# Reading the attention's stacked heads in sixteen-row pieces, and taking the combining weights' split one step earlier

## The chip, the cores and the metric

The kernel runs on one core of one Trainium2 chip. The metric is the device time of one execution in microseconds (us), lower is better. The program is one launch that computes two layers one after the other, so every stage's time adds to the total.

## The reference, cut to what matters

Eight batches of 512 tokens with 256 channels pass through four stages, each added to its input: an attention, a mixture of eight experts, a state-space block, and a second mixture of experts. The change touches the first and the last.

```python
xq, xk, xv = (x @ w.T + b).reshape(b, h, t, d)      # 16 heads of 16 channels, a reshape, not a transpose
xq, xk = rotate(xq), rotate(xk)                     # folded into the weights by the kernel
p = softmax(einsum('bhqd,bhkd->bhqk', xq, xk) / sqrt(d)); o = einsum('bhqk,bhkd->bhqd', p, xv)
...
p = softmax(maximum(x @ gate_W + gate_b, 1e-4))     # second mixture
w = maximum(p, 0.1) for the two best experts, divided by their sum
out = einsum('bsef,bse->bsf', einsum('bsd,edf->bsef', x, expert_W) + expert_b, w) / 2
```

## The kernel before, in words

Each engine runs one instruction stream; streams meet at semaphores, and an instruction that waits holds up all that stand behind it on its engine.

**Attention.** It runs in slots `t`, one for each of 32 tiles (a batch n has four; tile u = 4n + r holds four heads). Products of queries and keys are made of an upper and a lower part of each operand, three products in one matmul: a stack has 48 rows for each head pair, 16 rows each of "upper, lower, upper" against "lower, upper, upper". In slot t:

- SP, the queue that issues most transfers, first reads the stacks of tile t+3 (`load_stack`, which calls `read_stack` for two halves) when the transposed scores of slot t-1 are issued, then a tile of x (`load_rows`, L285), then stores the negated row maxima of tile t+1 (`load_maxima`, L318), waits for that store to land, and reads them into the stack (L322, two transfers). The scores of slot t+1 wait for these. Then it writes chunk t+8 of the projected queries or keys to the scratch tensor `scr` in HBM, an upper and a lower part (`write_scratch`, L263), each of 2048 pieces of 128 bytes. In every fourth slot a transfer of 512 KB of the residual follows (L379 or L340).
- TensorE takes the transposed scores of tile t (L928, sixteen matmuls), the scores of tile t+2 for the maxima (L937), the values, projections and transposes.
- VectorE takes the maxima (L670), ScalarE the exponentials (L523), GpSimd the splits into parts (L452, L454, L444, L446).

In slots -5 to -1 the same SP order holds for the first tiles; ACT issues half of tile 0's stack reads.

**Second mixture.** For each of eight batches there are 16 units, four token tiles by four pairs of experts. TensorE makes a unit in six matmuls of 512 columns (L1922) in one of four PSUM banks. Even units are weighed and added by VectorE (`accumulate`, L1820, two instructions), odd ones by ScalarE (L1684) and GpSimd (L1564). Unit u on an even bank may start when VectorE is done with unit u-4. Between its accumulations for batch n VectorE works out the combining weights of batch n+1, each step waiting for the one before: `shares` after unit 10, `share_parts` after unit 12. The result of `share_parts` is used by TensorE after unit 3 of batch n+1 (L1892), that of `shares` by ScalarE from unit 1 of it on.

```python
            for u in range(0, L.UNITS, 2):
                self.accumulate(n, u)
...
                else:
                    wait(pe, S["acc_done"], L.UNITS // 2 * n + u // 2 - 1)
```

Of the kernel before, what the change touches and what calls it, by code (L numbers as in the profile page):

```python
# [10 lines left out]
F32 = mybir.dt.float32  # L11
# [13 lines left out]
def wait(eng, sem, value):  # L25

    if not isinstance(value, int) or value > 0:
        eng.wait_ge(sem, value)
# [44 lines left out]
class Experts:  # L73
# [14 lines left out]
    def carve(self, k, at, shape, dt=F32, n=1):  # L88

        size = int(np.prod(shape[1:]))  # L90
        part = self.w[:, k:k + n, :] if dt == F32R else self.plain_pair[:, :, :] if n == 2 else self.plain[k][:, 0:1, :]
        flat = part.rearrange("p e c -> p (e c)")[:, at:at + size]
        names = ["a", "b", "c", "d"][:len(shape) - 1]
        return flat.rearrange(f"p ({' '.join(names)}) -> p {' '.join(names)}", **dict(zip(names, shape[1:])))
# [38 lines left out]
def attention_phase(nc, all_sems, A, x_out, route, experts):  # L133

    with ExitStack() as ctx:
# [30 lines left out]
        qst = carve(2, 0, [P, 4, 2, 512], F32R)  # L166
        kst = carve(3, 0, [P, 4, 2, 512], F32R)
# [22 lines left out]
        both, before = sb("both", [P, E0, 5]), sb("before", [P, E0, 5])  # L190
# [14 lines left out]
        scr = nc.dram_tensor("at_scr", (2, 2, 2, DK, NH, NJ, 32), F32, kind="Internal").ap()  # L205
# [16 lines left out]
        stack_ready = [sem(f"stack_ready{r}") for r in range(4)]  # L222
# [36 lines left out]
        def write_scratch(eng, q, kind):  # L259

            n, a = q // 4, q % 4
            to = scr[n % 2, a // 2, (kind + a // 2) % 2, :, :, 8 * (a % 2):8 * (a % 2) + 8, :].rearrange("d h j k -> j d h k")
            eng.dma_start(to, (qk_hi, qk_lo)[kind][:, q % 2, :].bitcast(F32)).then_inc(scr_written[n % 2][a % 2], 16)  # L263

        def read_stack(eng, u, half):

            r, n = u % 4, u // 4
            for b in range(2):
                eng.wait_ge(scr_written[n % 2][b], 64 * (n // 2 + 1))
            heads = slice(4 * r + 2 * half, 4 * r + 2 * half + 2)  # L270
            row = 64 * half
            for m, st, pair, single in ((0, qst, 16, 0), (1, kst, 0, 32)):
                both = scr[n % 2, m, :, :, heads].rearrange("s d h j k -> (s d) (h j k)")
                eng.dma_start(st[row + pair:row + pair + 32, r, :, :].bitcast(F32).rearrange("d h n -> d (h n)"), both).then_inc(stack_ready[r], 16)
                upper = scr[n % 2, m, m, :, heads].rearrange("d h j k -> d (h j k)")
                eng.dma_start(st[row + single:row + single + 16, r, :, :].bitcast(F32).rearrange("d h n -> d (h n)"), upper).then_inc(stack_ready[r], 16)

        def chunk_bank(q):
            return t_ps[:, q % 2, :] if q < 4 else f_ps[:, :]
# [1 line left out]
        def sync(sp):  # L281
# [22 lines left out]
            def load_stack(u):  # L304

                if u == 0:
                    sp.wait_ge(const_set, 5)
                wait(sp, t_ready, 16 * (u - 3))
                read_stack(sp, u, 0)
                if u:  # L310
                    read_stack(sp, u, 1)
# [13 lines left out]
            def write_chunk(q):  # L325

                n, a = q // 4, q % 4
                if a == 0:
                    for r in range(4):
                        wait(sp, stack_ready[r], 128 * (n - 1))  # L330
                sp.wait_ge(qk_hi_ready, q + 1)
                write_scratch(sp, q, 0)
                if q > 3:
                    sp.wait_ge(qk_lo_ready, q + 1)
                    write_scratch(sp, q, 1)
# [6 lines left out]
            for t in SLOTS:  # L342
# [8 lines left out]
                if (q := chunk(t)) is not None:  # L351
                    write_chunk(q)
                    if q == 3:
                        load_stack(0)
# [30 lines left out]
            for k in range(E0):  # L385
                at = sp.value_load(pad_row[0:1, k:k + 1], min_val=0, max_val=LIST - P)
# [107 lines left out]
        def scalar(act):  # L494
# [15 lines left out]
            def first_chunk(q):  # L510

                act.wait_ge(qk_ready, q + 1)
                if q > 1:
                    act.wait_ge(scr_written[0][q % 2], 32)
                act.activation(qk_hi[:, q % 2, :], qk[:, q % 2, :], ACT.Copy).then_inc(qk_hi_ready, 1)
                act.wait_ge(qk_lo_ready, q + 1)
                write_scratch(act, q, 1)
# [40 lines left out]
            for t in SLOTS:  # L558
# [5 lines left out]
                for k in range(16):  # L564
# [26 lines left out]
                    if k == 15 and t == -5:  # L591
                        read_stack(act, 0, 1)
# [321 lines left out]
        def tensor(pe):  # L914
            pe.wait_ge(ident_in, 16)

            def of_head(stack, r, h, rows, chunk=None):

                half = slice(64 * (h // 2), 64 * (h // 2) + rows)
                return stack[half, r, h % 2, :] if chunk is None else stack[half, r, h % 2, chunk * P:(chunk + 1) * P]  # L920
# [9 lines left out]
            def scores(u, m, a):  # L930

                if m == 0 and a == 1:
                    pe.wait_ge(stack_ready[u % 4], 128 * (u // 4 + 1))
                if a == 1:
                    wait(pe, max_done, 8 * u + m - 1)
                h, c = m // 4, m % 4
                last = pe.matmul(s_ps[:, m % 2, a, :], of_head(qst, u % 4, h + 2 * a, 48, c), of_head(kst, u % 4, h + 2 * a, 48), start=True, stop=True)  # L937
                if a == 0:
                    last.then_inc(s_ready, 1)
# [82 lines left out]
            for t in SLOTS:  # L1022
# [3 lines left out]
                for k in range(16):  # L1026
                    if tile(t) is not None:
                        scores_T(t, k)
                    if (u := tile(t + 2)) is not None:
                        scores(u, k // 2, 1 - k % 2)  # L1030
# [10 lines left out]
                    if k in (4, 6) and (n := batch(t, 10)) is not None:  # L1041
# [3 lines left out]
                        h = (k - 4) // 2  # L1045
# [24 lines left out]
            n = NB - 2  # L1070
# [366 lines left out]
class SecondExperts:  # L1437

    E, PAIRS, XB = 8, 4, 4
# [51 lines left out]
class SecondSync:  # L1491
# [21 lines left out]
    def body(self):  # L1513

        L, S, sp = self.L, self.L.S, self.sp
        for n in range(NB):
            sp.wait_ge(S["tile_done"], 4 * (n + 1))
            sp.dma_start(self.x_out[n * T:(n + 1) * T, :].rearrange("(k p) c -> p k c", p=P), L.x[n % L.XB][:, :, :]).then_inc(S["x_stored"], 16)
            if n + L.XB < NB:
                sp.wait_ge(S["x_stored"], 16 * (n + 1))  # L1520
                self.load(n + L.XB)
        sp.wait_ge(S["x_stored"], 16 * NB)
# [190 lines left out]
class SecondVector:  # L1713
# [73 lines left out]
    def shares(self, n):  # L1787

        L, S, dve, steps, E = self.L, self.L.S, self.dve, self.top_steps, self.L.E
        m0, m1, c, left = L.work  # L1790
        comb = L.comb[n % 2]
        wait(dve, S["odd_done"], L.UNITS * (n - 1))
        steps(dve.scalar_tensor_tensor(m1, L.p, 0.1, m0, ALU.max, ALU.mult))
        steps(dve.tensor_reduce(L.small[:, 0, :], m1, AX.X, ALU.add))
        steps(dve.reciprocal(L.small[:, 1, :], L.small[:, 0, :]))
        steps(dve.tensor_tensor(m1, m1, self.per_row(L.small[:, 1, :]), ALU.mult))
        dve.tensor_scalar(comb, m1, 0.5, None, ALU.mult).then_inc(S["comb_ready"], 1)

    def share_parts(self, n):

        L, S, dve, steps, E = self.L, self.L.S, self.dve, self.top_steps, self.L.E
        comb = L.comb[n % 2]
        upper, lower, again = (L.comb_3[:, :, r * E:(r + 1) * E] for r in range(3))
        dve.wait_ge(S["comb_ready"], n + 1)
        wait(dve, S["combT_ps"], n)
        steps(dve.tensor_copy(upper.bitcast(F32R), comb))
        dve.tensor_copy(again, upper)
        dve.tensor_tensor(lower, comb, upper, ALU.subtract).then_inc(S["comb_3_ready"], 1)
        assert steps.count == L.TOP_STEPS, steps.count
# [17 lines left out]
    def first_batch(self):  # L1827

        self.dve.wait_ge(self.L.S["const_in"], 48)
        self.scores(0)  # L1830
        self.first_choice(0)
        self.second_choice(0)
        self.shares(0)
        self.share_parts(0)

    def body(self):

        L, dve = self.L, self.dve
        for n in range(NB):
            dve.wait_ge(L.S["comb_ready"], n + 1)  # L1840
            for u in range(0, L.UNITS, 2):
                self.accumulate(n, u)
                if n + 2 < NB:
                    if u == 0:
                        self.variance(n + 2)
                    if u == 2:
                        self.newton(n + 2)
                if n + 1 < NB:
                    if u == 6:
                        self.scores(n + 1)  # L1850
                        self.first_choice(n + 1)
                    if u == 8:
                        self.second_choice(n + 1)
                    if u == 10:
                        self.shares(n + 1)
                    if u == 12:
                        self.share_parts(n + 1)


class SecondTensor:  # L1860
# [630 lines left out]
```

## Time and profile before

| what | value |
|---|---|
| median of 3 runs | 2147.16 us (2144.86 to 2148.03) |
| profiled execution, its own time | 2147.16 us |
| span from first to last instruction | 2145.3 us |
| mean granted TensorE clock | 0.94 |
| busy: TensorE, VectorE, ScalarE, GpSimd | 88%, 76%, 60%, 66% |

The time outside the span is 1.9 us. A share of busy time is a mean over four stages with different limits; what a change is worth has to be read in its own stage. Line numbers are those of the kernel printed above. SPq is SP's queue of transfer issues; its durations are the time that the issue took, not the transfer.

### The profile page before, as it was taken

The numbers are of one execution on the slowest core, as the hardware profiler recorded it, in microseconds if no ns is written. First come the engines' busy times: TensorE is split into PE (matmuls) and PEld (weight loads), VectorE is DVE, ScalarE is ACT, GpSimd is POOL, SyncE is SP. The second block draws the span as 40 slices with busy tenths as digits, with TensorE's granted clock in tenths as the row PEclk, the third lists the DMA queues.
The fourth block names the chain that finished last, engine by engine and source line by source line (L and its number), as shares of the span: only waits on it lengthen the run. The fifth ranks groups of instructions, "written<-read, shape, count | busy, mean of one in ns | idle before, by whom it ended". The sixth has DMA issues, their size and how long they took to land.

```text
span 2145.3 us, 32281 instructions
## 1 busy us (share of the span) xinstructions
PE 1894.8 (88%) x9878; PEld 1109.1 (52%) x9878; DVE 1641.0 (76%) x2274; ACT 1283.0 (60%) x2736; POOL 1421.8 (66%) x1198
## 2 busy tenths in 40 slices
PE   3699999999973999984799999999999999779998
PEld 2344444444433999982345353535454544247776
DVE  4688888787744655650699999999999999966664
ACT  3177666676662433335687777777777767734443
POOL 4344445542334344440699999999999999966665
PEclk8599999998885999996899999999999999999999
DMA  5666656555235454560404050405040404200100
GB/s 105 117 108 107 100 101 117 116 116 112 65 116 176 81 92 72 115 138 23 168 0 178 0 178 0 178 0 178 1 178 0 168 0 169 98 30 21 40 30 30
DMA packets 231395, 194.35 MB, mean 91 GB/s; under 512 B 147219, under 2 KB 200235, under 8 KB 230716
## 3 DMA queue, kind: packets, MB, share of 16 engines
q1 hardware_dynamic: 205498, 163.33, 28.9%
q0 software_dynamic: 13296, 17.77, 4.8%
q10 hardware_dynamic: 12434, 11.18, 1.9%
q8 instruction: 85, 1.39, 0.3%
q14 instruction: 82, 0.67, 0.1%
HBM read 138.15 MB, written 54.08 MB: 90 GB/s over the span
## 4 chain that ended last, share of the span: by engine, by line
POOL 34%; PE 12%; issue 7%; ACT 1%; DVE 1%; DMA 0%; POOLq 0%; DVEq 0%; ACTq 0%
POOL mb_dbu L2110 22%; POOL mb_hp L2116 10%; PE mb_da_ps L1922 9%; POOL mb_dtu L2122 1%; PE mb_f_ps L1883 1%; PE mb_f_ps L2352 1%; PE mb_f_ps L2370 0%; PE mb_y_ps L1901 0%; PE mb_f_ps L2356 0%; PE mb_f_ps L2360 0%; PE mb_f_ps L1872 0%; DVE mb_da_ps L2292 0%; DVE mb_hp L2290 0%; ACT mb_res L2186 0%; ACT mb_xin L2189 0%
## 5 line engine op out<-in xcount | busy, mean ns | idle before, releaser
L2110 POOL TENSOR_TENSOR mb_dbu<-mb_dtu,mb_bbc 128x1024 f32<-128x1024 f32 x256 | 598.8, 2363 | 3.6 <-DVE mb_hp L2290 1.5
L523 ACT ACTIVATE ex_plain<-at_t_ps 128x512 f32<-128x512 f32 x512 | 289.4, 595 | 175.0 <-PE at_t_ps L928 169.6
L2292 DVE TENSOR_TENSOR_SCAN mb_da_ps<-mb_da_ps,mb_dbu 128x1024 f32<-128x1024 f32 x160 | 365.4, 2284 | 4.6 <-ACT mb_da_ps L2164 3.3
L2333 PE MATMUL mb_y_ps<-mb_hc,lw_ident 128*128 128x512 f32 x640 | 311.4, 609 | 41.8 <-DVE mb_hc L2299 41.4
L670 DVE TENSOR_REDUCE at_mx<-at_s_ps 128x2 f32<-128x1024 f32 x256 | 310.6, 1218 | 35.0 <-PE at_s_ps L937 33.1
L937 PE MATMUL at_s_ps<-ex_w 48*128 48x512 f32 x512 | 226.4, 505 | 24.1 <-DVE at_mx L670 23.9
L928 PE MATMUL at_t_ps<-ex_w 64*128 64x512 f32 x512 | 219.0, 485 | 12.2 <-ACT ex_plain L523 7.0
L2116 POOL TENSOR_TENSOR mb_hp<-mb_hp,mb_cbc 128x1024 f32<-128x1024 f32 x96 | 226.5, 2359 | 0.0
L2290 DVE TENSOR_TENSOR_SCAN mb_hp<-mb_da_ps,mb_dbu 128x1024 f32<-128x1024 f32 x96 | 218.9, 2280 | 8.9 <-POOL mb_dbu L2110 6.3
L1309 POOL DMA_INDIRECT x<-m_o,m_xs x71 | 113.2, 1594 | 162.6 <-DMA x<-m_o,m_xs 88.3
L2333 PEld LDWEIGHTS mb_y_ps<-mb_hc,lw_ident 128*128 128x128 f32 x640 | 117.7, 191 | 199.4 <-issue 126.1
L2299 DVE TENSOR_TENSOR mb_hc<-mb_da_ps,mb_cbc 128x1024 f32<-128x1024 f32 x160 | 195.4, 1221 | 12.5
L2333 PE MATMUL mb_y_ps<-mb_hp,lw_ident 128*128 128x512 f32 x384 | 186.1, 608 | 15.6 <-POOL mb_hp L2116 15.6
L928 PEld LDWEIGHTS at_t_ps<-ex_w 64*128 64x128 f32 x512 | 86.4, 192 | 171.1 <-ACT ex_plain L523 125.9
L2163 ACT ACTIVATE mb_da_ps<-mb_dt,lw_a_neg 128x512 f32<-128x512 f32 x256 | 172.6, 674 | 0.0
L2164 ACT ACTIVATE mb_da_ps<-mb_dt,lw_a_neg 128x511 f32<-128x511 f32 x256 | 171.9, 672 | 0.0
L2162 ACT ACTIVATE mb_da_ps<-mb_zero 128x1 f32<-128x1 f32 x256 | 43.0, 168 | 204.1 <-DVE mb_hc L2299 162.4
L1414 PE MATMUL m_y_ps<-ex_w,m_xsT_hi 128*128 x568 | 157.0, 337 | 0.1
L948 PE MATMUL at_o_ps<-ex_plain 128*32 128x512 f32 x1024 | 144.6, 638 | 0.1
L1564 POOL TENSOR_TENSOR m_odd<-m_odd,m_odd_in 128x256 f32<-128x256 f32 x96 | 70.8, 737 | 95.7 <-ACT m_odd_in L1684 91.2
L2333 PEld LDWEIGHTS mb_y_ps<-mb_hp,lw_ident 128*128 128x128 f32 x384 | 73.6, 195 | 106.6 <-issue 76.5
L1820 DVE SCALAR_TENSOR_TENSOR m_x<-mb_da_ps,m_small,m_x 128x256 f32<-128x256 f32 x128 | 61.8, 483 | 81.0 <-PE mb_da_ps L1922 78.2
(354 smaller groups left out, 4088.6 us busy)
## 6 DMA issues: line engine op xcount, KB each, us to landing
mb_bbc<-mb_scr SPq DMA_DIRECT2D x64, 512.0 KB, 6.0
mb_cbc<-mb_scr SPq DMA_DIRECT2D x64, 512.0 KB, 6.0
ex_w<-at_scr SPq DMA_DIRECT2D x126, 128.0 KB, 3.6
m_xs<-rt_rows SPq DMA_DIRECT2D x71, 129.0 KB
at_scr<-at_qk_hi SPq DMA_DIRECT2D x32, 256.0 KB
ex_w<-at_scr SPq DMA_DIRECT2D x126, 64.0 KB, 3.6
at_scr<-at_qk_lo SPq DMA_DIRECT2D x28, 256.0 KB
at_xin<-in_x SPq DMA_DIRECT2D x32, 128.0 KB, 4.0
```

What stands on the lines that cost most here:

```text
L523: act.activation(probs[:, c, h, :], t_ps[:, k % 2, :], ACT.Exp, scale=SCALE).then_inc(exp_done, 1)
L670: dve.tensor_reduce(out, s_ps[:, m % 2, :, :], AX.X, ALU.max).then_inc(max_done, 1)
L928: pe.matmul(t_ps[:, k % 2, :], of_head(kst, r, h, 64, c), of_head(qst, r, h, 64), start=True, stop=True).then_inc(t_ready, 1)
L937: last = pe.matmul(s_ps[:, m % 2, a, :], of_head(qst, u % 4, h + 2 * a, 48, c), of_head(kst, u % 4, h + 2 * a, 48), start=True, stop=True)
L1922: last = pe.matmul(L.o_ps[:, u % 4, :], rows, w[:, e, kt, :], start=(m == 0), stop=(m == 5))
L2110: pool.tensor_tensor(dbu[:, q % 3, :, :], dtu_2, bbc[:, 2 * p:2 * p + 2, :], ALU.mult).then_inc(S["dbu_ready"], 1)
L2116: pool.tensor_tensor(hp[:, r, :, :], hp[:, r, :, :], cbc[:, 2 * p:2 * p + 2, :], ALU.mult).then_inc(S["hp_ready"], 1)
L2163: act.activation(da_ps[:, q % 2, 0, :], dt[:, d % 2, :], ACT.Exp, scale=a_neg[:, d, 2 * p:2 * p + 1])
L2290: dve.tensor_tensor_scan(hp[:, t % 3, :, :].rearrange("p j t -> p (j t)"), da, add, 0.0, ALU.mult, ALU.add).then_inc(S["scan_done"], 1)
L2292: dve.tensor_tensor_scan(da, da, add, 0.0, ALU.mult, ALU.add).then_inc(S["scan_done"], 1)
L2299: dve.tensor_tensor(hc[:, t % 2, :, :], da_ps[:, r, :, :], cbc[:, 2 * p:2 * p + 2, :], ALU.mult).then_inc(S["hc_ready"], 1)
L2333: last = pe.matmul(y_ps[:, v % 2, :], ident[:, :], src[:, j, :], start=False, stop=(q == tile_last[v] and j == 1))
```

## The change

Two edits. In the attention, the scratch tensor is laid out by part and operand, and each half of a tile's stacks is read by six transfers of 16 rows (64 KB) where four transfers were used before, two of 32 rows and two of 16. The rows, and the bytes, are the same; the key stack's order becomes "upper, upper, lower" and the query stack's "upper, lower, upper", which gives the same three products. The counts that TensorE and SP wait for rise from 128 to 192 for each tile. In the second mixture, the three instructions of `share_parts` are moved to the end of `shares`, so they stand before the accumulation of unit 12, not after it.

```diff
-            to = scr[n % 2, a // 2, (kind + a // 2) % 2, :, :, 8 * (a % 2):8 * (a % 2) + 8, :].rearrange("d h j k -> j d h k")
+            to = scr[n % 2, kind, a // 2, :, :, 8 * (a % 2):8 * (a % 2) + 8, :].rearrange("d h j k -> j d h k")
...
-            heads = slice(4 * r + 2 * half, 4 * r + 2 * half + 2)
-            row = 64 * half
-            for m, st, pair, single in ((0, qst, 16, 0), (1, kst, 0, 32)):
-                both = scr[n % 2, m, :, :, heads].rearrange("s d h j k -> (s d) (h j k)")
-                eng.dma_start(st[row + pair:row + pair + 32, r, :, :].bitcast(F32).rearrange("d h n -> d (h n)"), both).then_inc(stack_ready[r], 16)
-                upper = scr[n % 2, m, m, :, heads].rearrange("d h j k -> d (h j k)")
-                eng.dma_start(st[row + single:row + single + 16, r, :, :].bitcast(F32).rearrange("d h n -> d (h n)"), upper).then_inc(stack_ready[r], 16)
+            for kind, m, st, at in ((0, 0, qst, 0), (0, 0, qst, 32), (0, 1, kst, 0), (0, 1, kst, 16), (1, 0, qst, 16), (1, 1, kst, 32)):
+                row = 64 * half + at
+                eng.dma_start(st[row:row + 16, r, :, :].bitcast(F32).rearrange("d h n -> d (h n)"),
+                              scr[n % 2, kind, m, :, 4 * r + 2 * half:4 * r + 2 * half + 2].rearrange("d h j k -> d (h j k)")).then_inc(stack_ready[r], 16)
...
-                        wait(sp, stack_ready[r], 128 * (n - 1))
+                        wait(sp, stack_ready[r], 192 * (n - 1))
...
-                    pe.wait_ge(stack_ready[u % 4], 128 * (u // 4 + 1))
+                    pe.wait_ge(stack_ready[u % 4], 192 * (u // 4 + 1))
...
         dve.tensor_scalar(comb, m1, 0.5, None, ALU.mult).then_inc(S["comb_ready"], 1)
-
-    def share_parts(self, n):
-
-        L, S, dve, steps, E = self.L, self.L.S, self.dve, self.top_steps, self.L.E
-        comb = L.comb[n % 2]
-        upper, lower, again = (L.comb_3[:, :, r * E:(r + 1) * E] for r in range(3))
         dve.wait_ge(S["comb_ready"], n + 1)
         wait(dve, S["combT_ps"], n)
         steps(dve.tensor_copy(upper.bitcast(F32R), comb))
...
                     if u == 10:
                         self.shares(n + 1)
-                    if u == 12:
-                        self.share_parts(n + 1)
```

## Rows read from the trace of the kernel before

**Rows 1.** The four stages, by windows: busy time, clock, DMA share, GB/s
```profile
95.00:640.00 545.00, 506.03 (x4432) 230.09 (x4430) 420.55 (x712) 364.48 (x739) 234.90 (x357) 0.93 0.53 104
980.00:1925.00 945.00, 851.09 (x2257) 411.39 (x2258) 852.38 (x585) 684.89 (x1424) 872.07 (x455) 0.97 0.24 87
1925.00:2145.30 220.30, 213.17 (x1009) 169.37 (x1007) 134.64 (x387) 94.51 (x210) 132.17 (x167) 0.99 0.10 32
```

**Rows 2.** Waits of SP's queue, 95 to 510 us: total, times, longest
```profile
SPq L322 <- DMA at_nscr<-at_nm_parts: 84.3, 25, 5.0
SPq L274 <- PE at_t_ps L928: 32.1, 20, 3.5
SPq L263 <- POOL at_qk_hi L452: 28.7, 16, 5.2
```

**Rows 3.** Timeline of SP, slot 1: start us, us, what
```profile
112.16 1.77 SPq L274 DMA_DIRECT2D ex_w<-at_scr  x1
113.98 0.41 SPq L276 DMA_DIRECT2D ex_w<-at_scr  x1
...
116.75 0.42 SPq L276 DMA_DIRECT2D ex_w<-at_scr  x1
117.21 0.42 SPq L285 DMA_DIRECT2D at_xin<-in_x  x1
117.68 0.43 SPq L318 DMA_DIRECT2D at_nscr<-at_nm_parts  x1
121.19 0.52 SPq L322 DMA_DIRECT2D ex_w<-at_nscr  x2
```

**Rows 4.** Timeline of SP, a store of maxima with nothing ahead of it
```profile
589.32 0.32 SPq L318 DMA_DIRECT2D at_nscr<-at_nm_parts  x1
590.75 0.53 SPq L322 DMA_DIRECT2D ex_w<-at_nscr  x2
```

**Rows 5.** Timeline of SP: the reads of maxima in slots -1, 3, 4, 7
```profile
92.11 0.53 SPq L322 DMA_DIRECT2D ex_w<-at_nscr  x2
...
152.35 0.52 SPq L322 DMA_DIRECT2D ex_w<-at_nscr  x2
...
166.79 0.53 SPq L322 DMA_DIRECT2D ex_w<-at_nscr  x2
...
213.76 0.52 SPq L322 DMA_DIRECT2D ex_w<-at_nscr  x2
```

**Rows 6.** Timeline of PE: first transposed scores of slots 0, 4, 5, 8
```profile
95.00 0.40 PE L928 MATMUL at_t_ps<-ex_w 64*128 64x512 f32 x1
...
155.93 0.40 PE L928 MATMUL at_t_ps<-ex_w 64*128 64x512 f32 x1
...
170.60 0.40 PE L928 MATMUL at_t_ps<-ex_w 64*128 64x512 f32 x1
...
217.03 0.40 PE L928 MATMUL at_t_ps<-ex_w 64*128 64x512 f32 x1
```

**Rows 7.** Timeline of VectorE, second mixture, units 10 to 14 of batch 2
```profile
2005.09 0.18 DVE L1797 TENSOR_SCALAR m_small<-m_small 128x32 f32<-128x32 f32 x1
2005.18 1.00 DVE L1820 SCALAR_TENSOR_TENSOR m_x<-mb_da_ps,m_small,m_x 128x256 f32<-128x256 f32 x2
2006.10 0.51 DVE L1806 CAST m_small<-m_small 128x32 fp32r<-128x32 f32 x1
2006.64 0.18 DVE L1807 COPY m_small<-m_small 128x32 f32<-128x32 f32 x1
2006.74 0.19 DVE L1808 TENSOR_TENSOR m_small<-m_small 128x32 f32<-128x32 f32 x1
2006.84 1.00 DVE L1820 SCALAR_TENSOR_TENSOR m_x<-mb_da_ps,m_small,m_x 128x256 f32<-128x256 f32 x2
```

**Rows 8.** Timeline of GpSimd and PE in the same stretch
```profile
2005.09 0.78 POOL L1579 TENSOR_TENSOR m_x<-m_x,m_odd 128x256 f32<-128x256 f32 x1
2005.84 0.73 POOL L1564 TENSOR_TENSOR m_odd<-m_odd,m_odd_in 128x256 f32<-128x256 f32 x1
2006.94 0.39 PE L1922 MATMUL mb_da_ps<-lw_next_hi,m_xT_hi 128*128 128x512 f32 x1
```

**Rows 9.** Timeline: two small VectorE steps and the GpSimd operations beside them
```profile
1999.73 1.43 POOL L1571 TENSOR_TENSOR m_odd<-m_odd,m_bias 128x256 f32<-128x256 f32 x2
2000.07 0.44 DVE L1781 TENSOR_TENSOR m_small<-m_small 128x32 f32<-128x32 f32 x1
2000.55 0.66 DVE L1782 TENSOR_TENSOR m_small<-m_small 128x32 f32<-128x32 f32 x1
```

**Rows 10.** Timeline: VectorE's maxima and the matmul that waits for them
```profile
67.00 1.21 DVE L670 TENSOR_REDUCE at_mx<-at_s_ps 128x2 f32<-128x1024 f32 x1
68.26 0.79 PE L937 MATMUL at_s_ps<-ex_w 48*128 48x512 f32 x2 [0.67 <-DVE at_mx L670]
```

More of the change, by code:

```diff
@@ L1791, in shares @@
         comb = L.comb[n % 2]
+        upper, lower, again = (L.comb_3[:, :, r * E:(r + 1) * E] for r in range(3))
         wait(dve, S["odd_done"], L.UNITS * (n - 1))
@@ L1833, in first_batch @@
         self.shares(0)
-        self.share_parts(0)
     def body(self):
```

## The prediction

> **What bounds the kernel now.** I read the page by stage, then the windows. In the attention PE is busy 506 of 545 us, with VectorE next at 421; in the second mixture PE is busy 213 of 220 us and VectorE 135 [rows 1]. The stage between them, 945 us with GpSimd at 872, isn't touched. So each edit can only cost or gain what reaches PE in its own stage, and a microsecond there is one on the total, since the stages follow each other.
>
> Then the waits of SP's queue. In the attention SP waits 84 us for the landing of the stored maxima and only 32 us for PE, in 20 slots [rows 2]: it has about 1.6 us to spare in such a slot, of slots some 15 us long. The issues themselves stand in the timeline of SP. After a write of small pieces the first stack read takes 1.77 us to be issued, the other seven follow at 0.46 us each, from 113.98 to 117.21, then the tile of x and the store of maxima, and the read of the maxima goes 3.51 us after that store was issued [rows 3]. With nothing ahead of it the same store lets its reader go after 1.43 us [rows 4]. So about 2 us of the 3.5 are a queue of earlier transfers that is still draining, and not SP.
>
> Last, the timeline of the second mixture around units 10 to 14, below.
>
> **The stack reads.** The bytes and rows stay, so the transfers' own work stays; four more issues for each of 32 tiles are added, in all 128 (two of them on ACT's queue for tile 0, whose issues are the same size). The cost of one on SP is (117.21 - 113.98) / 7 = 0.46 us [rows 3], so 1.85 us for each tile and 59 us of SP's time. What stands behind them on SP is the tile of x, then the maxima, then the writes of queries and keys. The stacks themselves are read a whole slot ahead of their use, and no wait for them shows among the longest. The first that can be late are the maxima. Their reader is issued 2.9 us ahead of the first transposed scores of slot 0 (92.11 to 95.00), 3.6 us ahead in slot 4, 3.8 in slot 5 and 3.3 us in slot 8 [rows 5, 6]. By estimate such a read takes 2 us to land (1.43 us was seen for the store, which is a like size, plus its issue), which leaves margins of 0.9, 1.6, 1.8 and 1.3 us.
>
> How much later does the store land? Not at all, if the four issues only fill time in which the transfers ahead were draining anyway (2 us of queue against 1.85 us); 1.85 us, if nothing drains meanwhile. I take 0.8 us for a plain slot, nearer to full absorption because the queue seen is as long as the added issues, and 0.4 where a transfer of 512 KB stands ahead. These add up over slots in which SP has nothing to spare. Slots -2 and -1 give 1.6, and some 0.2 more comes from tile 0: 1.8 against a margin of 0.9, PE 0.9 us late. In slots 1 and 2 SP's spare time takes part of the lag back. In slots 3 and 4, with none left after the 512 KB transfer, it grows to some 3.7, against a margin of 1.8 (166.79 to 170.60, less 2) [rows 5, 6]: PE 1.9 us late. Slots 7 and 8 make it 5.2 against 2: 3.2 us. From slot 10 on SP waits for GpSimd too, up to 5.2 us at once [rows 2], and its lag is taken back. So +3 us. Bounds: 0 with full absorption, and, carrying 1.85 us a slot through the same sum, 15 us.
>
> **The split of the weights.** Nothing is added; three instructions, L1806 to L1808, go from behind the accumulation of unit 12 to ahead of it. What is queued behind them is that accumulation, and the one who waits for it is PE: unit 0 of the next batch takes the bank of unit 12. Now the accumulation starts at 2005.18 and ends at 2006.18, and PE starts that unit at 2006.94 with no gap [rows 7, 8]. From the end of a VectorE instruction to a matmul that waits for it is 68.26 - 68.21 = 0.05 us [rows 10]. So the accumulation has 0.7 us to spare.
>
> The price of the three in their new place depends on GpSimd. In the old place they take 0.74 us, from 2006.10 to 2006.84. The first of them shows 0.51 us for work that the second does in 0.18, and it ends when GpSimd's operation does (2005.84 + 0.73 = 2006.57) [rows 7, 8]. The same is seen before: two steps of 32 columns take 0.44 and 0.66 us beside GpSimd's two operations from 1999.73 to 2001.16, the second ending at 2001.21 [rows 9]. VectorE gets one such instruction in for each that GpSimd ends. In the new place GpSimd is busy without a gap from 2005.09 to 2006.57 [rows 8]. L1797 ends at 2005.27; L1806 can start 0.04 us on and is held to 2005.87 + 0.04 = 2005.91; L1807 waits for it and is held by the next operation to 2006.57 + 0.08 = 2006.65; L1808 starts 0.1 us behind and the accumulation 0.1 us behind that, at 2006.85. It ends at 2007.85, PE can go at 2007.90 and not at 2006.94: 0.96 us late. It happens in seven batches of eight (the last has no next one), the work on both sides is hung on PE, so the pattern repeats, and PE has no idle time to give it back: 7 x 0.96 = 6.7 us. Bounds: if only the first is held, the accumulation starts at 2006.15 and PE is 0.26 us late, 1.8 us in all; if none is, it starts at 2005.72, inside the margin, 0; with L1808 caught too, about 8 us. I take the middle case because L1781 and L1782 in the rows behave so.
>
> On this place the Trainium skill has a rule ("SBUF — State Buffer", Who interferes with whom): VectorE and GpSimd share a pair of ports under an exclusive lock, a copy or cast in a two-port mode and a two-input operation from SBUF contend for it, and the later one blocks fully. By that rule L1807, a copy, for which no row here shows a held case, can be held as L1806 is. If it can't be, the sum for this part would be the 1.8 us above. The trace agrees for the CAST, at 0.51 us.
>
> Sum: 3 + 6.7 = 10 us. The profiled execution took 2147.16 us, 1.9 more than its span, and equals the median of the runs; so 2157 us.
>
> **The rivals.** First, not slower: the three instructions slip between GpSimd's operations, as they would if the lead over GpSimd moved by half a microsecond, and the stack reads are absorbed. It decides at a shift of the accumulation below 0.7 us. For it: the issues are hidden in a draining queue, and PE shows no wait for VectorE in this stage. Against it: the GpSimd pair without a gap. Time 2147 to 2151.
>
> Second, SP becomes the bound in the first ten slots: each of the 1.85 us counts. For it: SP's mean wait for PE is 1.6 us, less than 1.85 [rows 2]. Against it: the 2 us of queue. That is 15 + 7 = 22 us, 2169. The Trainium skill ("DMA: Bandwidth & Descriptors", Rules for kernel authors) says to coalesce many small transfers, since under 64 KB one pays mostly overhead; these are 64 KB each, at that edge, and no run yet shows what a split costs.
>
> Third, faster: with more, smaller transfers the tile of x and the maxima find a shorter queue and land sooner, which would matter where VectorE waits for x in the start. They are issued later, though, so at most 1 or 2 us, and the second edit would have to cost nothing. Below 2143.
>
> **How the numbers follow.** Forecast as summed, some 2152 to 2163: 0.60. Not slower: 0.20. SP-bound: 0.12. Faster: 0.03. The rest, 0.05, is a second edit that costs more than a microsecond a batch. Predicted 2157. The range 2149 to 2167 leaves out the faster case, part of the first rival and most of the second. About 0.2%, 4.3 us, is what a measurement of this kernel can tell from no change: slower by more is 0.60 + 0.12 + 0.05, less a little for the low end of the forecast, 0.75; within it 0.22; faster 0.03.
>
> **What would show it.** The SP timeline: 12 reads at 0.46 us and the store of maxima answered in less than 3.5 us. The first transposed scores of slot 0 near 96, of slot 8 near 220. In the second mixture, L1806 and L1807 at 0.5 to 0.7 us each, the accumulation of unit 12 more than 1.5 us later against its unit, and a wait of PE for VectorE (L1820) seven times, about 1 us each; the stage 7 us longer than 220. The prediction is wrong if L1807 isn't held, if the stage's pattern shifts so that GpSimd's gap meets the three, or if PE in the attention is late by 10 us by slot 10.

## The result, and the profile after

The kernel with the change takes 2162.88 us, the median of four runs (2159.97 to 2164.84), against 2147.60 us for the kernel before in the same rounds (2144.86 to 2148.37). The ratio of the repeated runs is 1.0085, with a 95% interval of 1.0064 to 1.0104: slower by 0.85%, about 18 us (13.7 to 22.3). These medians alone differ by 15.3 us, 0.71%; all fourteen executions on record have a median of 2165.0 us. The profiled execution took 2161.31 us, with a span of 2159.5 us against 2145.3. The prediction had 2157 us, with a range of 2149 to 2167.

To place the 14.2 us of the span, the start of each instruction was compared with the start of the same instruction before. The transposes of the combining weights in the second mixture, the first of them before any unit there, are later by 8.1 us in batch 0, then by 9.0, 9.9, 10.7, 11.6, 12.4, 13.3 and 14.2. So 8.1 us come from what lies ahead and 6.0 from the second mixture. In the attention the first transposed scores are later by 1.4 us in slot 2, 1.7 in slot 3, 4.7 in slot 4, 8.0 in slot 5, and 8.1 in the last slot. Nothing is added between the attention and the second mixture. The 1.4 us of slot 2 are no sign of the change: kernels whose attention is untouched (e2_split, e6_split_latefinish and e9_latefinish, below) are 1.1 to 1.8 us late there too.

Windows of the changed kernel, for the attention, the state-space block and the second mixture, each edge moved by what its stage has shifted. The columns are those of [rows 1]: stretch and its length, then busy time and number of instructions of PE (TensorE's matmuls), PEld (its weight loads), VectorE, ScalarE and GpSimd, the granted clock of TensorE, the DMA share and GB/s.

```profile
95.00:648.00 553.00, 512.88 (x4436) 231.19 (x4435) 421.63 (x713) 364.41 (x739) 234.66 (x357) 0.92 0.53 103
980.00:1933.00 953.00, 850.61 (x2256) 411.07 (x2257) 852.58 (x586) 687.47 (x1429) 872.25 (x460) 0.97 0.24 86
1933.00:2159.50 226.50, 214.74 (x1010) 169.03 (x1008) 139.65 (x387) 94.62 (x210) 132.44 (x167) 1.00 0.09 31
```

Against [rows 1] the attention is 8 us longer. PE's busy time there grew by 6.9 us for the same matmuls (x4436 against x4432 of them in the records), and the granted clock fell from 0.93 to 0.92. That is a first sign that the loss isn't all waiting. The middle row's busy times are those of before, within 3 us. In the second mixture VectorE is busy 5.0 us more and PE 1.6 us, at full clock.

**The attention: SP's queue.** Its waits from 95 to 520 us (total, times, longest), to be read beside [rows 2]:

```profile
SPq L319 <- DMA at_nscr<-at_nm_parts: 66.8, 26, 4.4
SPq L272 <- PE at_t_ps L925: 30.0, 20, 3.3
SPq L263 <- POOL at_qk_hi L449: 14.5, 8, 4.0
```

The wait for the stored maxima fell by 17.5 us and that for GpSimd's upper parts by half: this is slack that was used up. The timeline of SP in slot 1, as [rows 3], and in slot 3 (the twelve reads are one row now, since they all stand on L272):

```profile
114.38 7.89 SPq L272 DMA_DIRECT2D ex_w<-at_scr  x12
122.32 0.42 SPq L282 DMA_DIRECT2D at_xin<-in_x  x1
122.78 0.43 SPq L315 DMA_DIRECT2D at_nscr<-at_nm_parts  x1
125.81 0.52 SPq L319 DMA_DIRECT2D ex_w<-at_nscr  x2
...
147.98 5.52 SPq L272 DMA_DIRECT2D ex_w<-at_scr  x12
153.54 0.42 SPq L282 DMA_DIRECT2D at_xin<-in_x  x1
154.06 0.38 SPq L315 DMA_DIRECT2D at_nscr<-at_nm_parts  x1
158.84 0.52 SPq L319 DMA_DIRECT2D ex_w<-at_nscr  x2
```

The second group gives the price of an issue: 5.56 us for twelve, 0.46 us each. The reader of the maxima is issued at 158.84; before it was at 152.35 [rows 5], 6.5 us earlier. The matmul that waits for it, in the timeline of PE (its last column is the idle time and who ended it):

```profile
96.81 0.79 PE L925 MATMUL at_t_ps<-ex_w 64*128 64x512 f32 x1 [0.18 <-DMA ex_w<-at_nscr]
...
143.02 0.50 PE L925 MATMUL at_t_ps<-ex_w 64*128 64x512 f32 x1 [0.20 <-DMA ex_w<-at_nscr]
...
160.65 0.78 PE L925 MATMUL at_t_ps<-ex_w 64*128 64x512 f32 x1 [3.13 <-DMA ex_w<-at_nscr]
```

These are the only three waits of PE for the maxima in the attention, 3.5 us in all; the long one is in slot 4. Before there is none. But 3.5 us is not 8. The rest stands in the second column of the last row: that matmul takes 0.78 us, where it took 0.40 at 155.93 before [rows 6]. Windows around it, of the changed kernel:

```profile
145.00:160.60 15.60, 12.22 (x131) 5.00 (x123) 11.41 (x16) 9.34 (x20) 5.90 (x12) 1.00 0.70 118
160.60:171.00 10.40, 9.94 (x36) 3.04 (x36) 5.30 (x9) 4.90 (x10) 0.73 (x2) 0.51 0.73 117
171.00:180.00 9.00, 8.87 (x110) 4.57 (x108) 7.01 (x8) 6.40 (x14) 5.97 (x10) 1.00 0.48 69
```

and of the kernel before, around the same work:

```profile
143.00:156.00 13.00, 12.69 (x134) 5.28 (x132) 10.82 (x15) 9.15 (x20) 5.88 (x13) 1.00 0.71 134
156.00:165.00 9.00, 8.56 (x47) 3.57 (x44) 7.72 (x11) 6.48 (x13) 1.21 (x3) 1.00 0.87 138
```

The granted clock after the wait of 3.13 us is 0.51 for 10.4 us, the lower of TensorE's two levels (1.2 and 2.4 GHz), where it stayed at 1.00 before. PE is busy there all the same (9.94 of 10.40 us), at half its speed: 10.4 x (1 - 0.51) = 5.1 us of its work at full clock is lost. Wait and clock make 3.1 + 5.1 = 8.2 us; from slot 2 to slot 5 the work fell 6.7 us behind (1.39 to 8.05), so the rest, 1.5 us, is likely to have gone into idle time that was there anyway. The Trainium skill ("TensorE: Matmul & The Clock Gate", What's actually happening) says that half rate is the default and activity lifts it. The trace agrees in part: 0.51 behind the idle stretch and 1.00 from 171 on. But PE is busy through nearly all of the slow stretch, so what lifted the clock at 171 and not sooner isn't seen here.

**The second mixture.** The timeline of GpSimd, VectorE and PE at unit 12 of batch 0, to be read beside [rows 7, 8]; the other six batches that have a next one show the same durations:

```profile
1959.74 0.78 POOL L1576 TENSOR_TENSOR m_x<-m_x,m_odd 128x256 f32<-128x256 f32 x1
1959.74 0.18 DVE L1795 TENSOR_SCALAR m_small<-m_small 128x32 f32<-128x32 f32 x1
1959.96 0.60 DVE L1798 CAST m_small<-m_small 128x32 fp32r<-128x32 f32 x1
1960.49 0.73 POOL L1561 TENSOR_TENSOR m_odd<-m_odd,m_odd_in 128x256 f32<-128x256 f32 x1
1960.60 0.66 DVE L1799 COPY m_small<-m_small 128x32 f32<-128x32 f32 x1
1961.17 0.18 DVE L1800 TENSOR_TENSOR m_small<-m_small 128x32 f32<-128x32 f32 x1
1961.28 2.10 DVE L1812 SCALAR_TENSOR_TENSOR m_x<-mb_da_ps,m_small,m_x 128x256 f32<-128x256 f32 x4
1962.41 0.47 PE L1911 MATMUL mb_da_ps<-lw_next_hi,m_xT_hi 128*128 128x512 f32 x1 [0.66 <-DVE m_x L1812]
```

L1798 to L1800 are the three moved instructions. The CAST ends at 1960.56, just behind GpSimd's operation (1960.52), and the COPY at 1961.26, just behind the next (1961.22). The waits of this stage name the price:

```profile
PEld mb_da_ps L1911 <- issue: 7.5, 7, 1.1
PE mb_da_ps L1911 <- DVE m_x L1812: 4.6, 7, 0.7
```

Seven times 0.66 us of waiting matmuls, and the weights' load ahead of each stands 1.1 us. The time from batch to batch went from 26.62 to 27.48 us, 0.86 us for each of seven.

### The profile page after: what moved, and what is told of

It reads as the page before. It is cut to its first block, busy times and chain, and to the rows that moved or that the text cites. A ratio compares the mean times of both kernels' runs of the same rounds, so it can differ in the third digit from the quotient of the medians.

```text
span 2159.5 us, 32409 instructions
## 1 busy us (share of the span) xinstructions
PE 1900.1 (88%) x9878; PEld 1108.3 (51%) x9878; DVE 1646.9 (76%) x2274; ACT 1283.0 (59%) x2736; POOL 1422.2 (66%) x1198
## 3 DMA queue, kind: packets, MB, share of 16 engines
q8 instruction: 85, 1.39, 0.3%
## 4 chain that ended last, share of the span: by engine, by line
POOL 33%; issue 8%; PE 7%; DVE 5%; ACT 1%; DMA 0%; POOLq 0%; DVEq 0%; ACTq 0%
POOL mb_dbu L2099 22%; POOL mb_hp L2105 10%; PE mb_da_ps L1911 4%; POOL mb_dtu L2111 1%; DVE m_x L1812 1%; PE mb_f_ps L1872 1%; PE mb_f_ps L2341 0%; PE mb_f_ps L2359 0%; DVE m_small L1755 0%; PE mb_f_ps L2345 0%; PE mb_f_ps L2349 0%; PE mb_f_ps L1861 0%; DVE m_small L1782 0%; DVE m_small L1779 0%; DVE m_small L1776 0%
```

## The experiments

Each run was timed in five rounds beside the kernel before on the same chip; the first four stood against 2151.69 us there, the next four against 2150.44, the last three against 2146.92.

### One edit at a time

**e1_reads** has only the new layout and the reads of 16 rows; **e2_split** has only this:

```diff
+        upper, lower, again = (L.comb_3[:, :, r * E:(r + 1) * E] for r in range(3))
...
         dve.wait_ge(S["comb_ready"], n + 1)
...
-                    if u == 12:
-                        self.share_parts(n + 1)
```

> The stack reads alone, on the kernel before. In the trace of the changed kernel PE is 8.1 us late by the fifth slot of the attention and stays so, and 6.0 us more are lost in the second mixture. Theory (the two edits act apart, and SP's issue of the maxima is what makes PE late in the attention): 8 us slower than the kernel before, within 2 us, all of it gained by slot 5, and the second mixture's stage as long as before. Rival (the edits need each other, or most of the loss is the split of the weights): under 4 us.

> The earlier split of the weights alone, on the kernel before. Theory (PE waits for the accumulation of unit 12 in seven batches, 0.86 us each): 6 us slower, within 2 us, with seven waits of PE for VectorE in the second mixture and nothing changed in the attention. Rival (the reads carry nearly all): under 2 us. Rival (the 0.96 us of the prediction): 6.7 us.

The reads alone took 2164.67 us (ratio 1.0063, 1.0042 to 1.0085), the split alone 2158.71 (1.0039, 1.0024 to 1.0054). Both edits cost, and the two together make 1.0102 against the 1.0085 of the whole, whose interval just holds it. The reads' 13.5 us (9 to 18) are more than the 8 that were expected of them. In the trace of e2_split the weights' transposes fall from 5.6 to 11.6 us behind over the second mixture, again 6.0 us, and in e1_reads they stay at 12.4. That e1_reads gains all its loss by slot 5 was wrong for its trace: the first transposed scores are 4.6 us late in slot 5 (after one wait for the maxima, 1.95 us), 7.4 in slot 6, 8.7 in slot 11 and 12.2 in the last slot.

The 5.6 us with which e2_split enters that stage don't come from its edit, since its attention is that of before. Windows of e2_split:

```profile
175.00:179.00 4.00, 2.77 (x17) 1.15 (x9) 3.31 (x6) 3.29 (x8) 2.61 (x5) 0.96 0.89 174
179.00:186.00 7.00, 7.00 (x23) 2.91 (x23) 3.96 (x8) 1.81 (x5) 0.00 (x0) 0.54 0.36 53
```

Here two waits for VectorE's maxima, 0.42 and 0.69 us, stand before a fall of the clock to 0.54. The kernel before has the same two waits, 0.42 and 0.70 us, and no fall. e6_split_latefinish and e9_latefinish, with the attention of before as well, show the same fall behind 0.42 or 0.43 and 0.69 or 0.70 us; e9_latefinish is 1.1 us late up to slot 5, 4.0 in slot 6, 5.1 in slot 11 and 5.7 in the last slot. So one trace of the attention carries some 5 us that differ between executions of the same instructions, and a shift in it counts only where a wait of its own stands beside it. By that measure 6.7 of the 8.1 us in the trace of the whole change are the reads', and of the 12.4 in e1_reads only the 3.1 of slots 3 to 5.

### The issues or the transfers?

**e3_tiny4** keeps the eight reads of before and adds four issues of 512 bytes to each tile; **e7_tiny2** adds two and **e8_tiny8** eight:

```diff
+            for i in range(2):      # for each half of a tile: 1 in e7_tiny2, 4 in e8_tiny8
+                eng.dma_start(tiny[u, half, i:i + 1, :], A["ident"][i:i + 1, :]).then_inc(stack_ready[r], 16)
```

> The kernel before with its own stack reads, and four issues more for each tile that move only 512 bytes each to a spare tensor; the counts waited for are those of the changed kernel. Theory (SP's issue time is the cost, 0.46 us each, whatever they move): the same 8 us as the sixteen-row reads, within 2.5 us. Rival (the cost is in the transfers, 16 rows a transfer being slower on the rings than 32): within 2 us of the kernel before.

> The kernel before with two more issues of 512 bytes per tile on SyncE's queue ahead of the store of the maxima (e3_tiny4 had four: 10.5 us slower by the median, ratio 1.0056). Theory A (idle time of SyncE's queue takes up the first issues, the rest reaches the reader of the maxima): two issues of 0.46 us, 0.9 us per tile, are mostly taken up: 1 to 3 us slower, the rise at slots 4 and 5 under 2 us instead of 5. Theory B (each issue costs in proportion, nothing is taken up): half of the four, 4 to 6 us slower.

> The kernel before with eight more issues of 512 bytes per tile. The queue of SyncE with two more of them answered the store of the maxima in 2.45 us on the mean of ten slots, with four in 2.32, against 3.90 before, so there is hardly anything left to take up. Theory A (a first 1.5 us per slot comes free because the store is answered sooner, and everything beyond it is paid in full): over e3_tiny4 each slot is 4 x 0.5 = 2 us longer wherever the chain of the maxima is the bound, 20 us in ten slots and more beyond: 30 us or more slower than before. Theory B (each issue costs in proportion, as two gave 5 and four 10 us by the medians): about 20 us slower than before.

Two took 2156.02 us (1.0024, 1.0011 to 1.0036), four 2162.13 (1.0056, 1.0034 to 1.0077), eight 2206.87 (1.0278, 1.0265 to 1.0291): 5, 12 and 60 us by the ratios. Four issues that carry 2 KB cost what the real reads' four more cost, within the intervals, so the issues are enough to explain the loss. The tiny ones are no exact stand-in, as each takes longer on the queue (the last section). In each timeline of SP, two distances were taken for the tiles 2 to 9 and averaged: from the first stack read to the store of the maxima, and from that store to its reader.

| kernel | first read to store | store to reader | sum |
|---|---|---|---|
| before | 5.63 us | 4.04 us | 9.67 us |
| with the change | 8.03 | 3.05 | 11.08 |
| e1_reads | 7.99 | 2.96 | 10.95 |
| e7_tiny2 | 7.12 | 2.59 | 9.71 |
| e3_tiny4 | 8.74 | 2.23 | 10.97 |
| e8_tiny8 | 11.83 | 1.96 | 13.79 |

What two tiny issues add ahead of the store (1.5 us) is given back in full by a store that is answered sooner; with four, 1.8 of 3.1 us; with eight, 2.1 of 6.2. On these means the answer isn't below 1.96 us. The first ten slots of e7_tiny2 are at most 0.5 us late, as theory A had it, but its ratio, 5 us, is above theory A's 1 to 3 and within theory B's 4 to 6. Its trace falls back from slot 16 on, 3.1 us there, where the granted clock is 0.70 and 0.62 in two windows of 5 us from 345, and is 9.5 us late in the last slot; PE waits nowhere for the maxima. So its cost isn't settled between the two. Eight cost more than both theories had (30 us or more, and 20) and show what was predicted as a rival for the change, SP as the bound: PE waits 17 times for the maxima, 38.9 us in all. A wait of PE in slot 3 of e8_tiny8 and the windows ahead of and behind it:

```profile
159.54 0.79 PE L931 MATMUL at_t_ps<-ex_w 64*128 64x512 f32 x1 [3.02 <-DMA ex_w<-at_nscr]
```

```profile
142.00:156.50 14.50, 13.94 (x137) 5.70 (x135) 12.24 (x16) 10.49 (x22) 6.00 (x9) 1.00 0.50 87
159.50:171.50 12.00, 11.53 (x39) 4.34 (x40) 6.19 (x9) 6.11 (x12) 0.72 (x2) 0.50 0.74 143
```

The same again: after 3.02 us without the maxima, 12 us at half clock. It isn't only this place. Behind all eleven waits of more than 2 us in e8_tiny8 the granted clock of the next 4 us is 0.50 to 0.71; behind the six shorter ones it is 1.00, but for one (1.57 us, then 0.60). One of either kind, behind a wait of 2.85 and of 1.95 us:

```profile
196.50:200.50 4.00, 4.00 (x14) 2.08 (x18) 0.77 (x2) 0.98 (x2) 1.37 (x3) 0.50 0.60 88
405.50:409.50 4.00, 4.00 (x23) 1.80 (x23) 2.18 (x6) 1.95 (x4) 0.00 (x0) 1.00 0.62 92
```

Across the kernels, from 155 to 175 us the clock fell in e1_reads (after a wait of 1.95 us), e3_tiny4 (2.06 us), e8_tiny8 and the kernel with the change, which all wait there for the maxima. It stayed at 1.00 in all eight other kernels with an edit and in the one before, which don't. How long it stays low differs: e1_reads lost about 1.7 us to it, the others about 5 or more. The shift from slot 2 to slot 5 goes with it: 6.7 us in the kernel with the change, 3.1 in e1_reads, 7.1 in e3_tiny4, 10.8 in e8_tiny8, and at most 0.1 in the eight.

### Issues moved behind the store

**e4_reads_behind** is e1_reads with the second half of the reads issued between the store of the maxima and the wait for it; **e5_before_behind** and **e11_behind_again** are the same order in the kernel before.

```diff
-                if u:
+                if u == 1:
                     read_stack(sp, u, 1)
...
+                if u + 2 < NT:
+                    read_stack(sp, u + 2, 1)
                 sp.wait_ge(nm_stored, 16 * (u + 1))
```

> The sixteen-row reads, with the second half of a tile's reads issued by SP between the store of the maxima and the wait for that store's landing, not ahead of the store. Theory (what counts is how late the maxima are issued; SP idles some 3 us in the wait, and six issues fit in there): the 8 us are given back, within 3 us of the kernel before. Rival (the transfers' own work on the rings): still 6 us or more slower. What could spoil it: the store's answer comes later because the reads share its rings; then the loss is only in part given back.

> The kernel before with its own eight reads of the score stack per tile; the second half of them is only issued later, between the store of the maxima and the wait that stands ahead of the read of the maxima. Theory A (SyncE's own issue time ahead of the store is what delays the maxima): four issues of 0.46 us fewer stand ahead of the store, so the maxima can only come earlier, by up to 1.8 us in slots 0, 4, 5 and 8, and nothing is added: 0 to 2 us faster, which reads as the same. Theory B (the number of transfers or the order in which they move sets the time): the second half now moves beside the store of the maxima and delays it, 2 to 8 us slower.

> The same kernel as e5_before_behind once more, since its gain (ratio 0.9982, 0.997 to 0.9995) is near what a measurement can tell. Theory A (the gain is real: each slot's reader is answered with 2.96 instead of 3.90 us, and the queue ahead of the store is 1 us shorter): 0.997 to 0.9995 again. Theory B (the gain was scatter, since GpSimd's last piece of the maxima now sets when the store may start): 0.9995 to 1.001.

With the order of e4_reads_behind the reads cost 1.0014 (0.9999 to 1.0029) in place of 1.0063; PE has no wait for the maxima any more, and the clock stays at 1.00 in slot 4. The number of transfers, their sizes and the layout are those of e1_reads, so they carry at most the 0.29% of this interval. The profiled execution of e4_reads_behind took 2161.09 us, near the slowest of its twelve (2149.45 to 2161.44): it is 2.6 us late in slot 5 and 12.0 in the last slot, with no wait for the maxima anywhere. So the reads' price rests on the timed ratios, and not on where a single trace ends. In the kernel before, the order gave 0.9982 (0.9970 to 0.9995) once and 1.0002 (0.9993 to 1.0011) the second time: a gain isn't confirmed. Its traces say why there is little to have. The waits of SP's queue in e5_before_behind, 95 to 520 us:

```profile
SPq L263 <- POOL at_qk_hi L454: 51.0, 18, 7.3
SPq L318 <- POOL at_nm_parts L448: 41.5, 24, 4.2
```

The store of the maxima now waits for GpSimd, which makes them, and no longer for its place in the queue; before, this wait was 6.2 us in four times. GpSimd's part had been hidden behind SP's queue.

### GpSimd taken from beside the copies

**e6_split_latefinish** is e2_split with GpSimd's finish of token tile 2 issued after unit 15 in place of unit 11, in the first seven batches; **e9_latefinish** has that alone, in the kernel before.

```diff
-                if u in (11, 15):
-                    self.add_bias(n, u // L.PAIRS)
-                    self.finish(n, u // L.PAIRS)
+                if u == 11 and n == NB - 1:
+                    self.add_bias(n, 2)
+                    self.finish(n, 2)
+                if u == 15:
+                    for k in range(2 if n < NB - 1 else 3, 4):
+                        self.add_bias(n, k)
+                        self.finish(n, k)
```

> The split of the weights alone (the run e2_split), and GpSimd's addition of the bias and its finish of tile 2 issued behind unit 15 instead of unit 11 in the first seven batches of the second mixture, so that GpSimd has nothing of them to do beside the three copies of the split. Theory A (the 0.86 us per batch are VectorE's two copies held while GpSimd works on the shared port, plus their own time): the two copies fall from 0.60 and 0.66 us to under 0.25 us each, TensorE's wait for the sum of unit 12 goes from 0.66 us to about zero, and the split costs at most 0.3 us per batch, 2 us in all against its control e9_latefinish. Theory B (the copies are only longer by the queue ahead of them and the price is three more instructions before the sum): the durations stay, and the split costs about 6 us as in e2_split.

> Control of e6_split_latefinish: the kernel before with GpSimd's addition and finish of tile 2 issued behind unit 15 instead of unit 11 in seven batches, and nothing else. Both theories: within 0.2% of before, since GpSimd has idle time behind unit 15; if it is slower, by more than 4 us, the finish is late for the store or the next tile, and e6 has to be read against this run instead of against before.

The control takes 1.0000 of before (0.9987 to 1.0012), the split beside it 1.0009 (0.9997 to 1.0021), in place of 1.0039. VectorE and GpSimd at the three instructions (L1805 to L1807 here), in e6_split_latefinish:

```profile
2011.36 0.18 DVE L1805 CAST m_small<-m_small 128x32 fp32r<-128x32 f32 x1
2011.57 0.72 DVE L1806 COPY m_small<-m_small 128x32 f32<-128x32 f32 x1
2012.21 0.18 DVE L1807 TENSOR_TENSOR m_small<-m_small 128x32 f32<-128x32 f32 x1
...
2011.52 0.74 POOL L1564 TENSOR_TENSOR m_odd<-m_odd,m_odd_in 128x256 f32<-128x256 f32 x1 [1.12 <-ACT m_odd_in L1688]
```

Here GpSimd rests for 1.12 us, and the CAST goes through in 0.18 us. The COPY meets the next operation, which began 0.05 us ahead of it, and is held for 0.72. With one held copy and not two, the time from batch to batch is 26.94 us against 26.62 in the control: 0.32 us, 2.2 us in all, and PE shows no wait of its matmuls for VectorE in the second mixture. Theory A holds in its size, 2.2 against at most 2; that both copies would be free was wrong.

### Both put right

**e10_both_repaired** is the whole change with the order of e4_reads_behind and that of e6_split_latefinish.

> The whole change, with the two orders tried one by one before: the second half of the stack reads issued behind the store of the maxima (as in e4_reads_behind, 1.0014), and GpSimd's addition and finish of tile 2 behind unit 15 (as in e6_split_latefinish, 1.0009). Theory A (the change costs what it does by two separate places, the issues ahead of the store and the held copies ahead of the sum of unit 12, and the two simply add): ratio to before near 1.002, about 5 us above before, and 10 us below the kernel with the change. Theory B (something else in the change, such as the other layout of the scratch, carries a part): it stays 8 us or more above before.

It took 2151.40 us, ratio 1.0017 (1.0007 to 1.0028), which is what the two parts add up to, 1.0023, within the interval. PE has no wait for the maxima in the attention, and its clock from 160.6 to 171 us is 1.00:

```profile
160.60:171.00 10.40, 10.08 (x118) 4.38 (x118) 8.84 (x13) 8.02 (x18) 5.23 (x6) 1.00 0.48 99
```

So by the middle values four fifths of the loss (0.85% against 0.17%) sat in two places, and everything else in the change, the layout of the scratch included, carries at most the rest. No kernel here beats the one before by more than can be measured.

## Why the prediction was right, and which terms were off

The direction, the two places and the split's price were worked out rightly. The total was not: 10 us were summed, against 15 by the medians and 18 by the ratio, and 2162.88 us lies at the very edge of "some 2152 to 2163". It is inside the range because the range had room for a reads' term some 10 us larger than the 3 that were summed, which is in part luck.

**The split: 6.7 us predicted, 6.0 measured.** Every step came as it was worked out from [rows 7 to 9]. The CAST took 0.60 us (0.60 was the sum), the COPY 0.66 (0.70), the bank was free later and PE stood seven times. The price was 0.86 us a batch and not 0.96. The accumulation starts 1.54 us behind the start of L1795 (1961.28 less 1959.74) where the sum had 1.76 for the same step, since L1800 begins ahead of the COPY's end (1961.17 against 1961.26) and not 0.1 us behind it; e6_split_latefinish gives the lower case too, 2.2 us for one held copy where 1.8 was the bound. The step taken on the likeness of L1781 and L1782 alone, that a COPY is held like the CAST, is shown. The Trainium skill ("SBUF — State Buffer", Who interferes with whom) says that a copy in a two-port mode contends with GpSimd for a shared pair of ports, and that the one that comes later blocks fully. The trace agrees: the COPY takes 0.66 us here and 0.72 in e6_split_latefinish, each until GpSimd's operation is about over, against 0.18 alone. The ports themselves aren't seen in a trace.

**The stack reads: 3 us predicted, 8.1 in the trace (6.7 of them beside a wait), 13.5 by the ratio of e1_reads.** The mechanism was right as far as it went: issues of SP ahead of the store (e3_tiny4), a part of them absorbed in a store answered sooner, the rest carried from slot to slot until PE waits for the maxima in slot 4. An issue cost 0.46 us as read from [rows 3], and the reads of the maxima landed in 1.8 to 2.0 us (158.84 to 160.65 the shortest), as estimated. Two terms of the sum were mis-sized.

- "I take 0.8 us for a plain slot": it was 11.08 - 9.67 = 1.41 us. The absorbed part was 0.99 us, close to the 1.05 that was taken. But 2.40 us, and not 1.85, were added ahead of the store. Besides the four issues (1.92 us), the first read, the one behind the write, takes 0.25 us longer, and 0.23 us more stand between the last read and the store, most of it in one slot. So the reader came 6.5 us later in slot 3 and 7.5 in slot 4 (174.24 against 166.79), where the prediction had some 3.7.
- PE's lateness was counted as a wait and nothing more. The waits were 3.5 us, near the 3 of the sum (1.95 in e1_reads). The 5.1 us of half clock behind the longest had no term, though the prediction read the clock of the stage [rows 1]. In this trace it is the larger of the two, and it is what failed in the step "So +3 us".

The first transposed scores of slot 0 came at 96.81, of slot 8 at 225.06, where some 96 and 220 were said. The 1.8 us of slot 0 have a wait of only 0.18 us in them, so the 0.9 us of waiting that were predicted there did not come. After slot 5 nothing came, where 3.2 us were predicted for slot 8. (That 3.2 used a margin of 2 us where [rows 5, 6] had given 1.3 for the slot; with 1.3 it would have been 3.9.) PE itself is later by then, so the reader, by 9.2 us in slot 7 (222.98 against 213.76), was in time for matmuls that are later by 8.0.

**The medians.** The trace gives 14.2 us, the medians 15.3 and the ratio 18. For the reads alone the ratio of 1.0063 is 13.5 us, with an interval of 9 to 18, more than the 8.1 of the trace of the whole change and twice the 6.7 that stand beside a wait. Order alone brought it to 1.0014 (e4_reads_behind), so most of it hangs on issues ahead of the store; but by which waits and spells of low clock the rest of it comes isn't shown. Low-clock spells that fall in other places in other executions, as in e2_split, may be that rest; it stays open.

**The rivals.** "SP becomes the bound" would have made 15 us in ten slots; it carried 1.85 us a slot, and 1.41 of the 2.40 us added survived, so the change stands nearer to it than to full absorption, and e8_tiny8 shows it come true, at 60 us. "Not slower" fell with the held COPY. Nothing became faster: the tile of x is issued later, at 122.32 in slot 1, not earlier.

## What to carry to other kernels

A queue that shows waits has slack only as far as its answer can still come sooner (here from 4.04 to 1.96 us); count added issues against that, slot by slot, and put those that aren't urgent behind the store and ahead of its wait. Where TensorE is the bound, price a new wait of a few microseconds by the clock behind it too: one of 3.1 us put the work 6.7 us back. A small VectorE copy costs what GpSimd is doing at that moment, so look at both timelines before moving one ahead of something that TensorE waits for.

## What was not expected of the hardware

An issue of 512 bytes on SP's queue costs no less than one of 64 KB: two take 1.21 us in e3_tiny4, 0.6 us each, against 0.46 us each.

```profile
168.77 1.21 SPq L279 DMA_DIRECT2D at_tiny<-in_ident  x2
```

The clock fell in some executions behind waits as short as 0.42 and 0.69 us in a row (e2_split), while the same waits left it at 1.00 in another (the kernel before).
